# Products of the identity matrix that nobody reads, issued on TensorE inside its waits at the start and the end of a four-layer graph network

## The reference

```python
# layer 0: attention with projected scores
e = leaky_relu((h @ W1) @ (h @ W2).T, 0.2); e = where(adj > 0, e, -1e12)
x = x + relu(softmax(e) @ (h @ W3))
# layers 1 and 3: graph attention, 4 heads of 64
q = h @ W;  e[i, j] = leaky_relu(dst[i] + src[j], 0.2), masked by adj
x = x + elu(softmax(e) @ q)
# layer 2: 4-head attention with masked scores, output projection, layernorm
out = softmax(mask(Q K^T / 8)) @ V;  out = layernorm(out @ Wo + bo) * gamma + beta
x = x + out
```

## Time and profile before

| | |
|---|---|
| median of 3 runs | 2969.06 us (2968.53 to 2969.58) |
| time of the profiled execution | 2968.62 us |
| its span, first to last instruction | 2966.8 us |
| TensorE busy, matmuls | 2859.6 us, 96% of the span |
| VectorE busy | 2128.6 us, 72% |
| ScalarE busy | 1681.5 us, 57% |
| GpSimd busy | 827.2 us, 28% |
| mean granted TensorE clock | 0.986 of full speed |

### The profile page before, as it was taken

How to read it: one execution, slowest core, us unless ns; L and a number is a source line. 1 busy time by engine, 2 the same in 40 slices (tenths; PEclk the granted TensorE clock), 3 DMA queues, 4 the chain that set the end, 5 groups by cost and what they waited for, 6 DMA issues and landing times.

```text
span 2966.8 us, 67544 instructions
## 1 busy us (share of the span) xinstructions
PE 2859.6 (96%) x27366; PEld 2006.1 (68%) x27366; DVE 2128.6 (72%) x5596; ACT 1681.5 (57%) x3554; POOL 827.2 (28%) x917
## 2 busy tenths in 40 slices
PE   5899999999999999999999999999999999999974
PEld 3667776767767667767667767666767666767653
DVE  4567877777877776877777877777787776787663
ACT  2546656556656655656655656655655655665642
POOL 2132222233222233232233222323222323232221
PEclk8999999999999999999999999999999999999987
DMA  3011011111011101011101011101011101001100
GB/s 101 9 36 37 30 44 44 29 38 40 28 44 44 37 30 44 23 44 44 38 29 44 23 44 44 44 23 44 25 43 44 44 23 44 32 28 37 37 16 29
DMA packets 58838, 109.86 MB, mean 37 GB/s; under 512 B 5568, under 2 KB 41408, under 8 KB 58528
## 3 DMA queue, kind: packets, MB, share of 16 engines
q1 hardware_dynamic: 58032, 104.61, 10.6%
q0 software_dynamic: 496, 0.92, 0.3%
HBM read 88.21 MB, written 17.30 MB: 36 GB/s over the span
## 4 chain that ended last, share of the span: by engine, by line
PE 78%; DVE 12%; POOL 6%; issue 2%; ACT 1%; DMA 1%; POOLq 0%; DVEq 0%; SPq 0%; ACTq 0%
PE ps L957 19%; PE ps L1058 11%; PE ps L1084 8%; PE ps L963 8%; PE ps L1093 8%; PE ps L1120 8%; PE ps L1014 8%; PE ps L948 4%; POOL rstd L361 3%; DVE stats L635 3%; POOL xc L411 2%; DVE pB L743 2%; PE ps L1002 2%; DVE nb L652 1%; DVE hn L819 1%
## 5 line engine op out<-in xcount | busy, mean ns | idle before, releaser
L383 POOL TENSOR_TENSOR qx<-qx,xc 128x512 f32<-128x512 f32 x128 | 163.4, 1277 | 883.8 <-ACT qx L523 883.8
L635 DVE BATCH_NORM_STATS2 stats<-xc 128x6 f32<-128x256 f32 x384 | 134.6, 413 | 328.5 <-POOL xc L393 264.1
L1058 PEld LDWEIGHTS ps<-vals,pA 128*64 128x64 f32 x8192 | 258.9, 140 | 73.9 <-issue 73.9
L442 ACT ACTIVATE hn<-xc,nb,rstd 128x256 f32<-128x256 f32 x384 | 209.1, 592 | 164.8 <-DVE nb L652 161.8
L1058 PE MATMUL ps<-vals,pA 128*64 128x65 f32 x8192 | 271.3, 225 | 21.5 <-DVE pA L743 21.5
L957 PE MATMUL ps<-wgat,hT 128*128 128x264 f32 x1024 | 273.1, 401 | 4.6 <-ACT hT L451 4.6
L1058 PE MATMUL ps<-vals,pB 128*64 128x65 f32 x8192 | 265.3, 223 | 4.4 <-DVE pB L743 4.3
L1058 PEld LDWEIGHTS ps<-vals,pB 128*64 128x64 f32 x8192 | 251.0, 138 | 20.9 <-issue 20.9
L451 ACT COPY hT<-ps 128x1024 f32<-128x1024 f32 x128 | 129.7, 1013 | 227.8 <-PE ps L948 223.6
L1084 PE MATMUL ps<-qx,qT 64*128 64x512 f32 x1024 | 249.8, 615 | 1.1 <-DVE hn L757 0.9
L358 POOL TENSOR_SCALAR rstd<-mv 128x4 f32<-128x4 f32 x160 | 74.9, 468 | 611.0 <-DVE mv L644 611.0
(11 more groups left out here) (141 smaller groups left out, 6103.5 us busy)
## 6 DMA issues: line engine op xcount, KB each, us to landing
qT<-r_dram SPq DMA_DIRECT2D x64, 512.0 KB, 4.0
hT<-r_dram SPq DMA_DIRECT2D x64, 512.0 KB, 4.9
x_in<-in_x SPq DMA_DIRECT2D x32, 512.0 KB, 3.9
out_x<-xc SPq DMA_DIRECT2D x32, 512.0 KB, 3.0
pX<-in_adj SPq DMA_DIRECT2D x1, 1024.0 KB, 8.0
r_dram<-growT SPq DMA_DIRECT2D x64, 8.0 KB, 1.3
pX<-in_L_gnn_W SPq DMA_DIRECT2D x2, 256.0 KB, 4.7
pA<-in_L_gnn_a POOLq DMA_DIRECT2D x8, 64.0 KB, 9.6
```

Source lines behind the costliest of these rows:

```text
L635: last = nc.vector.bn_stats(stats[s][:, t, :], src[:, t, :])
L1058: last = nc.tensor.matmul(ps[lo:hi, BANK[f"G{g}.{h}"], t * DV:(t + 1) * DV], gat_p[s][h % 2][:, j, t * P + lo:t * P + hi], vals[s][:, j, h ...
```

## The change

A helper `idle_turns(bank, count)` is added to TensorE's stream. Each of its turns multiplies the identity matrix by itself (128 x 128 weights, 128 columns, float32) into the first 128 columns of a bank that the next real step overwrites from its start or that holds nothing that is still wanted. Nothing reads these products. There are 369 of them, in eleven places: 34 and 6 in the first stage, 60 in slot 1, 12, 55 and 6 in the last but one slot, and 100, 6, 64, 13 and 13 in the last. No other engine's stream is changed, and no wait is added or taken away.

```diff
+            def idle_turns(bank, count):
+
+                for _ in range(count):
+                    nc.tensor.matmul(ps[:, bank, 0:P], ident[:, :], ident[:, :], start=True, stop=True)
...
             def slot(a, b, c, d):
+                if c is None:
+                    idle_turns(0, 60)
                 aggregate2(c, 0)
...
                 o_ready.wait(pe, c); u_columns(a, 0); v_rows(a, 0, 0); u_columns(a, 1)
+                if a is None and b is not None:
+                    idle_turns(BANK["G1.2"], 12)
                 gat_aggregate(b, 1, 2); gat_aggregate(b, 1, 3); scores0(a, 0)
...
-                masked0.wait(pe, a, 3); transposed(c, 3, 0); v_rows(a, 0, 1); transposed(c, 3, 1)
+                masked0.wait(pe, a, 3)
+                if a is None:
+                    idle_turns(6, 100 if b is None else 55)
+                transposed(c, 3, 0); v_rows(a, 0, 1); transposed(c, 3, 1)
                 transposed(c, 3, 2); v_rows(a, 0, 2); transposed(c, 3, 3); v_rows(a, 0, 3)
-                weights_transposed0(a, 0); q_rows(c, 3, 0); weights_transposed0(a, 1); q_rows(c, 3, 1)
+                weights_transposed0(a, 0)
+                if a is None:
+                    idle_turns(BANK["Q3.0"], 6)
+                q_rows(c, 3, 0); weights_transposed0(a, 1); q_rows(c, 3, 1)
...
-                v2_ready.wait(pe, b); gat_aggregate(c, 3, 0)
+                v2_ready.wait(pe, b)
+                if a is None and b is None:
+                    idle_turns(BANK["G3.0"], 64)
+                gat_aggregate(c, 3, 0)
...
-                qx_ready[1].wait(pe, a, 1); gat_aggregate(c, 3, 1); gat_max_across(a, 1)
+                qx_ready[1].wait(pe, a, 1)
+                if a is None and b is None:
+                    idle_turns(BANK["G3.1"], 13)
+                gat_aggregate(c, 3, 1); gat_max_across(a, 1)
...
-                pT2_act[0].wait(pe, b, 2); gat_aggregate(c, 3, 3)
+                pT2_act[0].wait(pe, b, 2)
+                if a is None and b is None:
+                    idle_turns(BANK["G3.3"], 13)
+                gat_aggregate(c, 3, 3)
...
-                bias_row(); poison(); agg0_norm.wait(pe, a, 4); pe.wait_ge(setup_ok, 6); transposed(a, 1, 0)
+                bias_row(); poison(); agg0_norm.wait(pe, a, 4); idle_turns(6, 34); pe.wait_ge(setup_ok, 6)
+                transposed(a, 1, 0)
                 transposed(a, 1, 1); transposed(a, 1, 2); transposed(a, 1, 3); pe.wait_ge(setup_ok, 5)
-                q_rows(a, 1, 0); q_rows(a, 1, 1); q_rows(a, 1, 2); q_rows(a, 1, 3)
+                idle_turns(6, 6); q_rows(a, 1, 0); q_rows(a, 1, 1); q_rows(a, 1, 2); q_rows(a, 1, 3)
```

## The result

The changed kernel takes 2980.74 us (median of 6 runs, 2979.43 to 2981.72) against 2969.32 us for the kernel before in the same runs: 11.4 us more, a ratio of 1.0037 with a 95% interval of 1.0024 to 1.005. The forecast was 2960.8 us, faster, and the time lies above its range. The profiled execution took 2979.43 us with a span of 2977.6.

The account below looks back on a forecast made before the run. TensorE was taken to bound the middle, with time lost to a half clock after waits at both ends. Kept clock 7.6 us plus 0.7 for other falls made 8.3, so 2969.06 - 8.3 = 2960.8 us, range 2956.0 to 2966.0.

Parts of the forecast that it names:

- the price of a turn: Every place with turns: 0.118 us each at full clock, taken from 24 transposes; 0.24 us at half clock.
- twelve products of `q_rows`: Last but one slot, behind the 55 and 6 turns: from 4.56 to 3.1 us, a saving of 1.5 us.
- None overruns: All places: every run of turns fits its wait, so the 369 turns cost nothing; without cover 43.5 us.
- rival "slower": Waits of the last slot and slot 1: turns don't hold the clock and overrun, 13 us slower, 2982 us; chance 0.04.
- rival "the change does nothing": Clock returns no sooner, or turns cost up to 0.194 us and overrun by 13.5 against 10.5 us; chance 0.06.
- The worth of a kept clock: Work behind the filled waits, both ends of the kernel: 10.5 us saved if every remaining pause is short enough.
- the 12 turns and the second 13: Last but one slot and end of last slot: saving 0, as other engines set the pace or the clock was full.
- Pauses: Waits left behind turns: 0.4 to 0.6 us should hold, 1.9 and 1.5 more likely hold, 2.2 to 2.6 more likely fall.
- the price of a fall: Work behind a short pause in which the clock falls: 3.66 - 2.09 = 1.57 us at most.
- Other falls: Short pauses the change does not fill: old falls may or may not happen, about half of one fall, 0.7 us gained.

Follow-up runs that it names:

- late_only: The changed kernel with the turns of the last slot alone (100, 6, 64, 13, 13), all other counts 0: 2978.15 us, ratio 1.0034 to the kernel before.
- transposes: The changed kernel with full counts, each turn a transpose of the identity instead of a product: 2958.52 us, ratio 0.9966 to the kernel before.
- half_counts: The changed kernel with every count of turns halved: 2958.98 us against 2968.66 for the kernel before, ratio 0.9966.
- fitted ones: The changed kernel with product counts 25, 4, 41, 8, 34, 61, 4, 42, 8, 8, worked out from 0.226 us a turn: 2961.45 us, ratio 0.9972.

## Why the prediction was wrong

**The term that failed is the price of a turn.** The prediction took 0.118 us from 24 transposes, with an upper bound of 0.194 us from a weight load without overlap. Measured: 0.226 us, outside both. The nearest row was the wrong kind: a float32 product runs as two passes, a transpose as one. The rows of the prediction would have told it. Four `q_rows` are eight `nc.tensor.matmul` calls in the code (4 row tiles x 2 tiles of features), and the earlier trace rows count 16 of them; I read the 16 and did not set it against the loop. The same miscount stands in "twelve products of `q_rows`" (six) and in the "64 products" of an aggregation, here and ahead of the prediction: `gat_aggregate` issues 32. No time depended on these, since like was compared with like. The transposes tell the other half: four `transposed` are 8 calls and 8 records.

**None overruns.** This followed from the price, and fell with it. By 0.226 us the 34, 60, 55, 100 and 64 turns and each 13 are 7.7, 13.6, 12.4, 22.6, 14.5 and 2.9 us in waits of 5.9, 9.7, 8.0, 14.2, 9.8 and 2.15. The rival "slower" named the point from which the sign turns, 0.142 us a turn in the wait of 14.2, and a result near it, 2982 us. Its mechanism was not the one at work: the clock held inside the 60 and the 100 turns, and the fall inside the 64 cost 1.6 us (16.19 against 14.56 in late_only). That the number came near is luck. The real one was that of the rival "the change does nothing" with a dearer turn. Put into the prediction's own sum, 0.226 us gives overruns of 1.8, 3.9, 4.4, 8.4, 4.7, twice 0.8 and some 0.8 for the sixes, 25.6 us, less 10.5: 15 us slower, where 11.4 were measured. (That rival's own 13.5 us, at 0.194 us a turn, counts only one of the two groups of 13, 0.4 us each.) An overrun costs less than its excess, because the transposes behind the 55 and the 100 turns no longer wait for ScalarE's row tiles: they pass in 1.04 us in one go, where before they were spread over 2.6 us in the one place and took 2.07 in the other.

**The worth of a kept clock was right.** Predicted 4.1 us for four `q_rows`, measured 3.75; predicted 2.4 us in slot 1, M1 to M2 gives 2.7; predicted 2.09 us for the aggregations, measured 2.09. That the 12 turns and the second 13 save nothing was not tested one by one; without the former the ratio did not get worse. With the price halved (transposes) the forecast of 8.3 us compares with 10.1 measured, inside its range of 3.1 to 13.

**Pauses.** Predicted: pauses of 0.4 to 0.6 hold, 1.9 and 1.5 more likely hold, 2.2 to 2.6 more likely fall. In half_counts and transposes, those of 1.84 and 1.97 us in the first stage held (transposes in 1.09 us), one of 4.20 cost the aggregation 1.2 us, one of 2.61 cost the `q_rows` the same, one of 2.90 cost them 1.3, one of 2.71 held. Later kernels blur it: behind pauses of 1.72 and 1.86 us the clock held, behind 1.98, 2.01 and 2.37 it fell. The rule of thumb was fair, though near 2 us it tells little, and so was the price of a fall: 1.48 us at most in these (3.57 against 2.09), where the prediction had 1.57.

**Other falls.** I gave 0.7 us to falls at short pauses elsewhere that might vanish. The one at the projection of the last but one slot came in every kernel that did not fill it, and after the change it cost 1.0 us more, 9.58 us for the 16 passes against 8.55 in the timeline of before:

```profile
...
2855.76 8.55 PE L963 MATMUL ps<-hT,wqkvo 128*128 128x512 f32 x16 [0.81 <-ACT hT L451]
...
```

**Not foreseen:** that the turns have to be fetched and so move the packets that lengthen a write on the chain (above), that passes of half the columns left a fallen clock at half, and that behind the small steps the clock also fell in full waits. In some executions it fell as the 60 or the 64 turns began or up to 1.2 us later, and they took about 1.6 us longer. Why it fell there in some executions and not in others is open.

## What to carry to other kernels

Count the records of a group against the loop that issues them before taking a duration from it: passes per operation depend on type and kind, and for float32 here a product is two and a transpose one. A pause that the filler work leaves in a wait costs at most one fall, 1.5 us here, while too much costs nearly all of its excess. So cover two thirds to four fifths of the wait rather than all of it: half the counts gained as much as fitted ones, and the full counts lost more than that gain. Use the finest grain that keeps the clock; here that is a transpose, and no kernel with transposes was slower than its twin with products. Filling the small steps ahead of a long stretch took 1.7 us out of that stretch, but the time of the whole kernel did not show it clear of noise.

## What the runs showed of the hardware

- A float32 product is two passes (738 records for 369), a transpose one (369 for 369). At full clock a pass with 128 weight columns takes 0.113 us with 128 moving columns (120 in 13.56 us) and 0.115 with 64 (68 in 7.80). With more it is dearer: 0.234 us with 264 (16 in 3.75) and 0.446 with 512 (16 in 7.13).
- Transposes of the identity held the full clock, 1.00 over 100 of them, and it came back to full inside a run of 60.
- Unbroken passes with 64 columns kept a full clock for 12 us in one place. In two others it fell about 2 us after they began, and it stayed at half to their end, for up to 38 us, where passes with 128 columns had 1.00. What tells the places apart was not tried.
- Added instructions bring packets of the instruction queue, 218 before and 223 after. A write of 8 KB takes 1.3 us, and up to 3.6 us when such a packet falls into it: so in all 229 long writes of 832, in 13 profiles. The time of the whole kernel shows no such write clear of noise.
